# Load pieces of 48, 5 and 3 rows, a power two steps apart, and three, five and five of the expert work on DVE, ACT and POOL, in a two-layer metaformer kernel

## The reference, cut to what matters

```python
# layer 0, expert layer: t is x as (32, 3136, 128)
probs = softmax(ln(t) @ router_w + router_b)
top_p, top_i = top_k(probs, 2);  top_p /= sum(top_p)
t = t + sum over the two chosen experts of top_p * (ln(t) @ expert_w[e] + expert_b[e])
# layer 1, focal modulation
y = ln(x) @ Wf + bf                  # q, context, four gates
ctx_all = gated sum of three depthwise convolutions and a mean
x = x + ((LayerNorm(q * (ctx_all @ Wh + bh)) * gamma + beta) @ Wp + bp)
```

## Time and profile before

| | us |
|---|---|
| runs | 12997.03, 13002.87, 13009.24 (median 13002.87) |
| profiled execution, its own time | 13003.63 |
| its span | 13001.8 |
| expert stage, about | 1860 to 4020 |
| focal input stage, about | 4020 to 6560 |
| convolution stage, about | 6560 to 8430 |
| focal output stage, about | 8430 to 11150 |
| recurrence, about | 11150 to 13001 |

### The profile page before, as it was taken

One profiled execution on the slowest core, in us unless ns is written; L12 is line 12 of the kernel. 1 busy time (PEld: TensorE's weight loads), 2 busy tenths in 40 slices (PEclk: granted clock), 3 DMA queues, 4 the chain that ended last, 5 costly groups with the idle time before them and its releaser, 6 DMA issues. The chain is left out here.

```text
span 13001.8 us, 325709 instructions
## 1 busy us (share of the span) xinstructions
PE 8644.4 (66%) x109727; PEld 5499.5 (42%) x109727; DVE 6469.0 (50%) x21703; ACT 4556.1 (35%) x12677; POOL 5573.7 (43%) x6829
## 2 busy tenths in 40 slices
PE   8999988888883222222269999834444444788888
PEld 6777753333332111111135555423333333455554
DVE  8999988888884111111125555523333333222222
ACT  5666655555552211111223333312222222233333
POOL 8888877777773111111112222112222222444444
PEclk9999999999997666666689999966666666899999
DMA  1222211111111111111144444322222222122222
GB/s 54 58 58 58 57 53 49 49 49 49 49 49 41 65 64 64 64 64 64 64 143 157 157 156 156 121 73 78 78 79 79 79 79 70 51 56 56 57 56 54
DMA packets 795890, 960.00 MB, mean 74 GB/s; under 512 B 321322, under 2 KB 660075, under 8 KB 771820
## 3 DMA queue, kind: packets, MB, share of 16 engines
q1 hardware_dynamic: 795500, 956.24, 23.5%
HBM read 576.90 MB, written 455.45 MB: 79 GB/s over the span
## 5 line engine op out<-in xcount | busy, mean ns | idle before, releaser
L944 PE MATMUL moe_pe_out<-moe_we,moe_xnT 128*128 128x512 f32 x3136 | 1535.7, 624 | 369.4 <-DVE moe_odd L837 195.9
L1248 PE MATMUL foc_px<-foc_idn,foc_xn 112*128 112x112 f32 x896 | 145.7, 292 | 1930.2 <-POOL foc_xn L1106 1864.6
L1920 PE MATMUL mod_pz<-mod_wpx,mod_yT 128*112 128x129 f32 x1792 | 478.9, 365 | 1377.2 <-DVE mod_xin L1824 1376.7
L1544 PE MATMUL conv_pc<-conv_c,conv_toep 128*128 128x432 f32 (+1 forms) x3584 | 1371.0, 535 | 0.0
L741 ACT ACTIVATE moe_scaled<-moe_pe_out,moe_gate 128x128 f32<-128x128 f32 x3136 | 891.9, 367 | 867.3 <-PE moe_pe_out L944 865.5
L1185 DVE BATCH_NORM_STATS2 foc_stat<-foc_xin 112x6 f32<-112x128 f32 x896 | 191.0, 276 | 1865.4 <-DMA foc_xin<-x 1865.4
L1750 ACT ACTIVATE mod_z<-mod_xin,mod_nmean,mod_rstd 112x128 f32<-112x128 f32 x896 | 368.9, 483 | 1996.2 <-DVE mod_nmean L1851 1947.1
L944 PEld LDWEIGHTS moe_pe_out<-moe_we,moe_xnT 128*128 128x128 f32 x3136 | 558.2, 195 | 1187.9 <-issue 1187.2
L2100 ACT ACTIVATE rec_yT<-rec_ph 128x32 f32<-128x32 f32 x3136 | 618.3, 197 | 1240.2 <-PE rec_ph L2221 1240.2
L1106 POOL TENSOR_SCALAR foc_xn<-foc_xin,foc_rstd,foc_nmean 112x127 f32<-112x127 f32 x448 | 202.5, 462 | 1886.2 <-DVE foc_nmean L1198 1884.4
L1406 POOL TENSOR_TENSOR conv_g<-conv_c,conv_gate 128x896 f32<-128x896 f32 x128 | 365.5, 2855 | 1474.6 <-DVE conv_out L1507 1371.0
(11 more groups left out here) (202 smaller groups left out, 21764.3 us busy)
## 6 DMA issues: line engine op xcount, KB each, us to landing
conv_toep<-rows_dram SPq DMA_DIRECT2D x32, 2304.0 KB, 14.0
c<-foc_cs SPq DMA_DIRECT2D x32, 1856.0 KB, 7.2
conv_cin<-c SPq DMA_DIRECT2D x32, 1856.0 KB, 9.0
ctx_all<-conv_out SPq DMA_DIRECT2D x32, 1792.0 KB, 6.5
att_xin<-x_windows SPq DMA_DIRECT2D x512, 98.0 KB
x<-att_x1s SPq DMA_DIRECT2D x1024, 49.0 KB
moe_xin<-x SPq DMA_DIRECT2D x112, 448.0 KB, 3.6
x<-moe_acc SPq DMA_DIRECT2D x112, 448.0 KB, 2.7
```

The lines of the kernel that those rows point to most:

```text
L944: ins = pe.matmul(pe_out[:, b, half, :], xnT[:, n.slot(2), t, :], we[:, half * 4:half * 4 + 4, :].rearrange("d e c -> d (e c)"), start=Tru ...
L1544: ins = pe.matmul(pc[k][:, half, 0:HALF * wide].rearrange("p (b i) -> p b i", i=wide)[:, :, i0:i1], w, tile[:, b, i0 + away:i1 + away], st ...
L1920: pe.matmul(pz[0:TOK, b, t, 0:C + 1], tile_of(yT, m, c, t), wpx[:], start=True, stop=True)
```

## The change

Expert stage: `MIX` goes from 4 to 3 and `TP` from 5 to 3. DVE's mix of expert 3 goes to ACT, which does it last, after a wait for DVE's three mixes of the tile. POOL adds the fifth scaled expert with one more add behind `join`, and normalises three tiles, in tiles 1, 3 and 5; ACT normalises the other four, one each in tiles 3 to 6. ACT waits for `others_ready` in place of `paired_ready` before it overwrites `scaled`.

`load_quads`: the pieces of each half are 48, 5 and 3 rows, six DMAs in place of four, and the waits for them count 6.

Focal output stage: the variance of x, its power, `negate`, `norm_z` and the gram matrix run one step later. On DVE `y_mean`, `negate` (now n-2), `y_mean_square`, `x_variance` (now n-1) and `y_variance` all stand between `gate` and `residual`. On POOL `roots` n+1 stands before the bias add of n+2.

```diff
-    TP = 5
+    TP = 3
-        scaled = S.sb("scaled", [P, 2, 4, C])
+        scaled = S.sb("scaled", [P, 2, 5, C])
+        quad = S.sb("quad", [P, 2, C])
-        MIX = 4
+        MIX = 3
...
-                pool.tensor_tensor(others[:, b, :], paired[:, b, 0, :], paired[:, b, 1, :], ALU.add)\
-                    .then_inc(others_ready, 1)
+                pool.tensor_tensor(quad[:, b, :], paired[:, b, 0, :], paired[:, b, 1, :], ALU.add).then_inc(quad_ready, 1)
+
+            def join_fifth(n, t):
+                b = (n.off * T + t) % 2
+                pool.wait_ge(quad_ready, n.val(T, t + 1))
+                pool.tensor_tensor(others[:, b, :], quad[:, b, :], scaled[:, b, 4, :], ALU.add).then_inc(others_ready, 1)
...
-                    if 1 <= t <= TP and last < -2:
-                        norm(n + 2, t - 1)
+                    if t in (1, 3, 5) and last < -2:
+                        norm(n + 2, t // 2)
                     join(n, t, first)
                     if t == 0 and last < -2:
                         scale(n + 2, first + 2)
                         hold(pool, turned[1], n.val(1, 1), ticks)
+                    join_fifth(n, t)
...
-                    act.wait_ge(paired_ready, n.val(T, t - 1))
+                    act.wait_ge(others_ready, n.val(T, t - 1))
...
-                for e in range(4):
-                    g = gate[:, n.slot(2), t, 4 + e:5 + e]
-                    ins = act.activation(scaled[:, b, e, :], pe_out[:, b, 1, e * C:(e + 1) * C], ACT.Identity, scale=g)
+                for e in (4, 5, 6, 7, 3):
+                    if e == MIX:
+                        hold(act, mixing, n.val(T * MIX, MIX * (t + 1)), ticks)
+                    half, at = divmod(e, 4)
+                    ins = act.activation(scaled[:, b, e - MIX, :], pe_out[:, b, half, at * C:(at + 1) * C], ACT.Identity,
+                                         scale=gate[:, n.slot(2), t, e:e + 1])
...
-                    if t == 4 and last < -2:
-                        norm(n + 2)
+                    if t >= TP and last < -2:
+                        norm(n + 2, t, t + 1)
...
-                hold(dve, mixing, n.val(T * MIX, MIX * t + 1), ticks)
-                gated(n, t, 3, odd[:, b, :])
+                hold(dve, mixing, n.val(T * MIX, MIX * t + 2), ticks)
+                gated(n, t, 2, acc[:, n.slot(4), t, :])
                 route_between(n, t, 3, more)
                 if first >= 1 or t >= 1:
                     add_others(n, t - 1)
-                route_between(n, t, 4, more)
-                hold(dve, mixing, n.val(T * MIX, MIX * t + 2), ticks)
-                gated(n, t, 2, acc[:, n.slot(4), t, :])
-                route_between(n, t, 5, more)
+                for place in (4, 5):
+                    route_between(n, t, place, more)
...
-        for row, real, rows in ((IMG - SHIFT, 0, SHIFT), (0, SHIFT, IMG - SHIFT)):
+        for row, real, rows in ((0, SHIFT, 48), (48, SHIFT + 48, 5), (IMG - SHIFT, 0, SHIFT)):
...
             def roots(n, first):
 
-                if first >= 3:
-                    hold(pool, z_normed, n.val(1, -2), ticks)
+                if first >= 4:
+                    hold(pool, z_normed, n.val(1, -3), ticks)
...
-                if last < -2:
-                    add_bias(n + 2)
                 roots(n + 1, first + 1)
+                if last < -2:
+                    add_bias(n + 2)
...
-                if first >= 1:
-                    norm_z(n - 1, first - 1)
+                if first >= 2:
+                    norm_z(n - 2, first - 2)
...
                 if last < -9:
                     gate(n + 9, first + 9)
-                if first >= 1:
-                    negate(n - 1, first - 1)
-                residual(n)
                 if last < -1:
                     y_mean(n + 1)
-                x_parts(n)
+                if first >= 2:
+                    negate(n - 2, first - 2)
                 if last < -1:
                     y_mean_square(n + 1)
+                if first >= 1:
+                    ins = x_variance(n - 1)
+                if last < -1:
+                    ins = y_variance(n + 1)
+                ins.then_inc(varied, 1)
+                residual(n)
+                x_parts(n)
                 x_statistics(n)
-                if last < -1:
-                    y_variance(n + 1)
-                x_variance(n)
...
-                if first >= 2:
-                    gram_of(n - 2, first - 2, last - 2)
+                if first >= 3:
+                    gram_of(n - 3, first - 3, last - 3)
```

More of the change, by code:

```diff
@@ L614, in expert_stage @@
         mixing, joined, mixed = S.sem("mixing"), S.sem("joined"), S.sem("mixed")
-        scaled_ready, paired_ready, others_ready = S.sem("scaled_ready"), S.sem("paired_ready"), S.sem("others_ready")
+        scaled_ready, paired_ready, quad_ready, others_ready = (S.sem(k) for k in ("scaled_ready", "paired_ready", "quad_ready", "others_ready"))
         x2_out = S.sems("x2_out", 4)
@@ L715, in front, with norm @@
                     act.activation(xnT[:, n.slot(2), t0:t1, :], px[:, b, 0:(t1 - t0) * P], ACT.Copy).then_inc(xT_out[b], 1)
-            def norm(n):
+            def norm(n, t0, t1):
                 a = n.slot(2)
                 hold(act, nmean_done, n.val(1, 1), ticks)
-                for t in range(TP, T):
+                for t in range(t0, t1):
                     ins = act.activation(xn[:, a, t, 0:C - 1], xin[:, n.slot(4), t, 0:C - 1], ACT.Identity,
                                          bias=nmean[:, a, t:t + 1], scale=rstd[:, a, t:t + 1])
-                ins.then_inc(normed_act, 1)
+                if t1 == T:
+                    ins.then_inc(normed_act, 1)
             def shares(n):
@@ L746, in step @@
                     act.wait_ge(filled, 2)
-                    norm(n)
-                    norm(n + 1)
+                    norm(n, TP, T)
+                    norm(n + 1, TP, T)
                     front(n, 0)
@@ L939, in experts @@
                 if first >= 1 or t >= 2:
-                    hold(pe, mixing, n.val(T * 4, 4 * (t - 1)), ticks)
+                    hold(pe, mixing, n.val(T * MIX, MIX * (t - 1)), ticks)
                     hold(pe, scaled_ready, n.val(T, t - 1), ticks)
@@ L1178, in layer_stats @@
                 if c == 0:
-                    hold(dve, x_in[m.slot(2)], m.turn(2, 16 * 4, 16 * 4), ticks)
+                    hold(dve, x_in[m.slot(2)], m.turn(2, 16 * 6, 16 * 6), ticks)
                 if first >= 7:
@@ L1702, in add_bias @@
                 if c == 0:
-                    pool.wait_ge(x_in[m.slot(2)], m.turn(2, 16 * 4, 16 * 4))
+                    pool.wait_ge(x_in[m.slot(2)], m.turn(2, 16 * 6, 16 * 6))
                 x = xin[:, m.slot(2), GRP * c:GRP * c + GRP, :]
@@ L1717, in step @@
                     add_bias(n)
+                    roots(n, 0)
                     add_bias(n + 1)
-                    roots(n, 0)
+                roots(n + 1, first + 1)
                 if last < -2:
                     add_bias(n + 2)
-                roots(n + 1, first + 1)
+                if last == -1:
+                    roots(n + 2, first + 2)
             run_steps(pool, N, U, step, AHEAD)
@@ L1747, in norm_z @@
                     hold(act, gram_added, n.val(1, -1), ticks)
-                b, r = n.slot(2), (n + 1).slot(2)
+                b = n.slot(2)
                 for t in range(GRP):
                     ins = act.activation(z[:, b, t, 0:C], xin[:, m.slot(2), GRP * c + t, :], ACT.Identity,
-                                         bias=nmean[:, b, t:t + 1], scale=rstd[:, r, GRP + t:GRP + t + 1])
+                                         bias=nmean[:, b, t:t + 1], scale=rstd[:, b, GRP + t:GRP + t + 1])
                 ins.then_inc(z_normed, 1)
@@ L1763, in step @@
                     square(n + 8)
-                if first >= 1:
+                if first >= 2:
+                    norm_z(n - 2, first - 2)
+                if last == -1:
                     norm_z(n - 1, first - 1)
-                if last == -1:
                     norm_z(n, first)
@@ L1842, in x_variance @@
                 hold(dve, stats, n.val(1, 1), ticks)
-                dve.tensor_scalar(var[:, (n + 1).slot(2), GRP:2 * GRP], mv[:, n.slot(2), :, 1], EPS_T, None, ALU.add)\
-                   .then_inc(varied, 1)
+                return dve.tensor_scalar(var[:, n.slot(2), GRP:2 * GRP], mv[:, n.slot(2), :, 1], EPS_T, None, ALU.add)
             def negate(n, first):
                 b = n.slot(2)
-                hold(dve, rstd_done, n.val(1, 2), ticks)
+                hold(dve, rstd_done, n.val(1, 3), ticks)
                 if first >= 2:
@@ L1863, in step @@
                     gate(n + 9, first + 9)
-                if first >= 1:
-                    negate(n - 1, first - 1)
-                residual(n)
                 if last < -1:
                     y_mean(n + 1)
-                x_parts(n)
+                if first >= 2:
+                    negate(n - 2, first - 2)
```

(15 more changed lines are left out.)

2 lines of the change are left out of this document (1 added, 1 removed).

## The result

The changed kernel takes 10957.94 us (median of four runs, 10947.03 to 10966.79) against 13003.25 us for the kernel before in the same session: a ratio of 0.843, 95% interval 0.841 to 0.844. The forecast was 10180 us, with a range to 10480. The direction was right, the time was not: 778 us too low.

What follows compares the result with a forecast made beforehand. DVE and PE were taken as near their limits in the expert stage, slow one-engine loads as bounding the focal stages. 13003.6 - 1683 - 1272 + 90 + 40 = 10179, about 10180 us; range 9930 to 10480.

Steps and rivals of the forecast that it cites:

- a slow load on one engine: Focal loads: 53-row pieces run on one DMA engine; new pieces gain 1683 us at input and 1272 at output.
- then 3.8 us for 1568 KB: Focal input load: its bytes take 3.8 us at 416 GB/s, landing at 15.3 us, for a period of 25.0 us.
- I take the q store's, the nearest whole tile: Focal input load: the new pieces were assumed to move at the q store's rate, 416 GB/s.
- the bound of 30: Focal input: slow bound, a period of 30 us if each small piece and issue adds a microsecond, -155 us.
- Rival 1: Focal input still waits for DMA, small pieces and six issues queueing on few engines: period 32 us, 10400 us; chance 0.10.
- +0.85 us on the loop: Focal output: four small DVE operations move between gate and residual, making the step 6.3 us against 5.9, 90 us lost.
- Gain 1302 - 30: Focal output: POOL's wait for `mod_xin` goes except 30 us at the first image, a gain of 1272 us.
- Rival 2: Focal output loop runs at PE's low clock level: 7.4 us a step, +245, 10425 us; chance 0.10.
- +0.35 us net per group: Expert stage: the new chain's waits outweigh DVE's saved mixes by 0.35 us over 112 groups, 40 us lost.
- 7 x 0.341 = 2.4 us won: Expert stage: DVE loses one mix of 0.341 us per tile, winning 2.4 us per group of seven tiles.
- The bound of 200 lost: Expert stage: the slow bound, 200 us lost, with some 80 us of blocked DVE adds left inside it.
- rival 3: All better: experts win 200 us and the input period is near 20 us (-150): 9830 us; chance 0.06.

Runs made afterwards that it cites:

- without expert 3: Changed kernel without ACT's scaling of expert 3 and its wait, that share left out, POOL's fifth add taking another expert's tile: 10455.76 us.
- Two repairs: Changed kernel with ACT's token copies ahead of expert 3's scaling at tile 0: 10863.85 us; with a separate semaphore for expert 3: 10842.44; with both: 10504.87.

## Why the prediction was right or wrong

**Part 1, a slow load on one engine: right.** The wide piece spreads: the loads' share is 0.97 where it was 0.06. The loads alone bring 2677 us, and `mod_xin`'s wait fell to 32.6 us where 30 was said.

**Part 1, "then 3.8 us for 1568 KB": wrong, 213 us.** The step that failed is "I take the q store's, the nearest whole tile". That is a store of 112 partitions at 416 GB/s; the load's wide pieces cover 48 partitions each. At 168 GB/s its 1568 KB take 9.6 us. The period became 33.4 us, outside the bound of 30. Rival 1 (32 us) had the size and part of the reason. By DVE's wait in the stage (394.6 us with six pieces, 287.2 with two of 56 rows, 209.6 with one of 112), 107 us lie with the narrow pieces and the further issues, as that rival had it, and 78 with loading one half at a time, which nothing in the prediction foresaw. One piece comes close to the 182 of the forecast. The steps between these kernels change the number of DMAs and their width at once, so this division is rough.

**Part 2, "+0.85 us on the loop": right in size; the output stage was missed by 92 us.** The small operations hold the residual for 0.88 us, of which `negate` had stood there before. Over the loop a step of the changed kernel is (9059.9 - 7510.5) / 223 = 6.95 us, 6.44 with only the loads: 0.51 for the 0.4 said (116 us for 90). The step itself was put at 6.3 us, from a burst of seven; the sum used only the difference. The other 66 us are in "Gain 1302 - 30", and this is the step that failed: it took POOL's wait for the stage's loss. The wait did go, but the stage gave back less than POOL had waited. POOL stood 41.07 us before it added the bias, and DVE, which still had work of the step before, stood 38.52:

```profile
9601.10 0.98 DVE L1851 SCALAR_TENSOR_TENSOR mod_nmean<-mod_mv,mod_rstd 112x4 f32<-112x4 f32 x1 [38.52 <-POOL mod_rstd L1713]
```

Over all images from the second on, POOL stood 1302.0 - 80.2 = 1222 us and DVE 1141. Without POOL's waits a step of the kernel before comes to (11119.7 - 8528.0 - 1222) / 223 = 6.14 us, and the loop with only the loads ran at 6.44. PE's busy time in the two loops is the same (1169 and 1170 us), so the clock did not make this difference. Rival 2 (7.4 us at the low level) came in part: 6.95 us at a mean clock of 0.75. L1851's stall did go, as said, and its operation takes 152 ns for 566 in the loads-only kernel, but moving it behind the residual would have been enough.

**Part 3, "+0.35 us net per group": wrong, 458 us, the largest miss.** The chain was named rightly, from DVE's third mix over ACT and POOL to `add_others`, and DVE waits in it 523.6 us. Three terms of the step failed. "7 x 0.341 = 2.4 us won" did not come: 10455.76 without expert 3, 10447.67 with the whole old stage. What is queued behind ACT's new wait was left out: I followed the chain to DVE and not to PE, whose router stands 283.9 us for the copies and whose matmuls stand 285.6 us for `moe_scaled`. And PE's clock went from 0.97 to 0.91, 184 us of its busy time, in no term. The bound of 200 lost took in none of these. The blocked adds of the earlier trace rows came, beside the pair add as in that row and hardly beside the fifth: `add_others` takes 486 ns on average for 401 in the changed kernel (66 us) and 611 without expert 3 (164 us). How much of that reached the stage's time stays open. With only the norms divided anew it takes 493 ns, and that kernel lost nothing.

One sum is off: rival 3 takes 200 for the experts off a forecast that already holds 40 lost, so its time should read 10180 - 240 - 150 = 9790 us, not 9830. Nothing else hangs on it.

## What to carry to other kernels

A new wait is priced by everything queued behind it on its engine, followed to every engine that needs it, and work taken off an engine may win nothing: here mixes of 267 us left DVE, its busy time fell by 62 and 25 us, and even with nobody doing them the stage was no faster. In both loops here longer waits of PE came with a lower granted clock, so that a wait cost more than itself; putting small operations behind the one that the loop needs brought 245 and 364 us for less than 1 us a step. A load's rate is taken from a transfer over the same partitions in the same direction, not from the fastest in sight.

## What the runs showed of the hardware

- Loads of x ran at 168, 199, 251 and 287 GB/s with widest pieces of 48, 56, 96 and 112 partitions, at busy shares of 0.88 to 1.06, and the store of 112 partitions at 401. A share near 1.00 doesn't tell the rate.
- Two repairs gave 94 and 115 us alone and 453 together; PE's granted clock was 0.91 with either and 0.96 with both.
- With five small operations of 0.88 us taken from between gate and residual, the step went from 6.95 to 5.30 us over the loop, while PE's granted clock went from 0.75 to 0.94.
- DVE's add of two SBUF tiles (128x128) takes 0.28 us alone, 0.29 beside POOL's norm and some 0.7 when POOL's pair add is running as it starts.
